# Moving the input normalisation of a gated recurrence from VectorE to ScalarE, with its statistics one step ahead

## What is computed

```python
h = layernorm(x) * (1 + ca) + sa
u = h @ W_in + b_in
gate_x, gate_a = sigmoid(u @ W_gx + b_gx), sigmoid(u @ W_ga + b_ga)
log_a = -8.0 * gate_a * softplus(a_param)
a, scale = exp(log_a), sqrt(1 - exp(2 * log_a))
# along the sequence: h_t = a_t * h_(t-1) + scale_t * gate_x_t * u_t
x = x + ga * (h @ W_out + b_out)
h = layernorm(x) * (1 + cb) + sb
x = x + gb * experts(h)
```

## Time and profile before

| | before |
|---|---|
| median of 3 runs | 1151.97 us (1151.54 to 1152.62) |
| the profiled execution, its own time | 1154.08 us |
| its span (first to last instruction) | 1152.3 us |
| PE busy | 1069.4 us, 93% |
| DVE / ACT / POOL busy | 746.0 / 759.1 / 430.4 us |
| mean granted TensorE clock | 0.962 |

### The profile page before, as it was taken

The page is one execution under the profiler, slowest core; times in us unless marked ns, Lnnn a source line. Parts: engine busy times, 40 slices in busy tenths (PEclk is TensorE's granted clock), DMA queues, the critical chain, the costliest instruction groups (busy, mean ns, idle before and its releaser), DMA issues.

```text
span 1152.3 us, 18801 instructions
## 1 busy us (share of the span) xinstructions
PE 1069.4 (93%) x6986; PEld 943.6 (82%) x6986; DVE 746.0 (65%) x1744; ACT 759.1 (66%) x1196; POOL 430.4 (37%) x387
## 2 busy tenths in 40 slices
PE   7899899999948999989999999999999999999993
PEld 6777777877736888879998899889998899888883
DVE  4779879989837888885535545354544554456565
ACT  4665647667427778877657776677667766776661
POOL 2121112112131445445445444445354444534532
PEclk8999989999867999999999999999999999999997
DMA  6035424121028445544434323433244332468971
GB/s 224 0 94 200 146 74 113 38 74 38 19 75 130 116 116 148 125 111 124 117 47 83 81 53 74 87 81 90 43 96 71 82 87 40 86 184 262 270 280 73
DMA packets 88442, 122.45 MB, mean 106 GB/s; under 512 B 17056, under 2 KB 74016, under 8 KB 87328
## 3 DMA queue, kind: packets, MB, share of 16 engines
q1 hardware_dynamic: 62960, 84.11, 23.2%
q0 software_dynamic: 24576, 36.37, 17.7%
q10 hardware_dynamic: 816, 0.79, 0.2%
HBM read 78.96 MB, written 42.27 MB: 105 GB/s over the span
## 4 chain that ended last, share of the span: by engine, by line
PE 59%; DVE 6%; ACT 2%; issue 2%; POOL 1%; DMA 0%; POOLq 0%; ACTq 0%; DVEq 0%
PE psum L1806 29%; PE psum L1831 26%; PE psum L1782 2%; DVE w_raw L1650 1%; DVE hidT L1696 1%; DVE scratch L1654 1%; PE psum L420 1%; DVE w L1644 1%; ACT rows_in L1587 1%; ACT hf L1610 1%; POOL out_x L1517 1%; DVE place L402 0%; ACT acc L1569 0%; DVE res_t L1654 0%; DMA out_x<-scratch 0%
## 5 line engine op out<-in xcount | busy, mean ns | idle before, releaser
L1806 PE MATMUL psum<-w,hidT 128*128 128x256 f32 x3072 | 375.1, 284 | 11.3 <-DVE hidT L1696 11.3
L1806 PEld LDWEIGHTS psum<-w,hidT 128*128 128x128 f32 x3072 | 367.3, 192 | 13.3 <-DVE hidT L1696 13.0
L1831 PE MATMUL psum<-xT,w 128*128 128x512 f32 x1536 | 372.2, 398 | 0.3 <-DVE xT L1683 0.3
L1696 DVE TENSOR_TENSOR hidT<-hf,hidT 128x512 fp32r<-128x512 f32 x256 | 175.4, 691 | 260.4 <-ACT hidT L1614 260.3
L1831 PEld LDWEIGHTS psum<-xT,w 128*128 128x128 f32 x1536 | 285.7, 190 | 59.7 <-DVE xT L1683 0.7
L1489 POOL DMA_INDIRECT ffn_rows<-rows_y,idx_cur x120 | 206.5, 1721 | 227.4 <-issue 167.8
L440 POOL DMA_INDIRECT rows_in<-x_rows,idx_cur x128 | 139.1, 1087 | 187.3 <-DVE idx_cur L413 152.7
L1558 ACT ACTIVATE rows_y<-psum,g_cur 128x256 f32<-128x256 f32 x128 | 53.8, 470 | 191.2 <-PE psum L1806 191.2
L1614 ACT ACTIVATE hidT<-hf 128x512 fp32r<-128x512 f32 x256 | 161.8, 632 | 8.1
L1610 ACT ACTIVATE hf<-psum 128x512 f32<-128x512 f32 x256 | 151.0, 590 | 22.1 <-PE psum L1831 13.1
L694 POOL TENSOR_SCALAR ve<-x 128x4 f32<-128x4 f32 x16 | 3.7, 229 | 221.3 <-DVE x L841 221.3
(11 more groups left out here) (205 smaller groups left out, 1238.9 us busy)
## 6 DMA issues: line engine op xcount, KB each, us to landing
w_raw<-in_L_ffn_w SPq DMA_DIRECT2D x30, 1024.0 KB, 6.0
x_rows<-x SPq DMA_DIRECT2D x16, 516.0 KB, 4.0
x_buf<-in_L_attn_x SPq DMA_DIRECT2D x16, 512.0 KB, 5.9
ffn_rows<-scratch SPq DMA_DIRECT2D x8, 1024.0 KB, 8.3
w_raw<-ffn_rows SPq DMA_DIRECT2D x16, 512.0 KB, 9.3
scratch<-x_rows SPq DMA_DIRECT2D x12, 512.0 KB, 7.1
out_x<-scratch SPq DMA_DIRECT2D x12, 512.0 KB, 4.2
rows_in<-x_rows,idx_cur POOLq DMA_INDIRECT x136, 2.9
```

The lines of the kernel that those rows point to most:

```text
L1696: dve.tensor_tensor(hidT[1][:, m, :], hf[m % HF][:], hidT[0][:, m, :].bitcast(F32), ALU.subtract).then_inc(f_hl, 1)
L1806: ins = pe.matmul(y_tile(u, t), hidT[qs][:, k, t * P:(t + 1) * P], w2_s[n % 2][qm][:, k, :], start=(x_ == 0), stop=(x_ == len(terms) - 1))
L1831: ins = pe.matmul(H_bank[m % 4], w1_s[n % 2][qs][:, k, m * P:(m + 1) * P], xT[qm][:, k, :], start=(x_ == 0), stop=(x_ == len(terms) - 1))
```

## The change

From group 5 on (`ON_DVE = 5`) the rows are normalised by ACT in place of DVE: four ACTIVATE Identity of 128x256 with scale rstd and bias -mean*rstd, after `keep_x1T` and before `gate_a` of the step whose group a it is. The statistics of such a group are taken one step earlier, in the same place of the DVE step; step 4 takes those of groups 4 and 5, step 15 none. POOL's `rstd1` moves with them and gets two more instructions, for the bias. SP loads group s+2 in step s, and there are six x buffers. The new tiles `nm1` are 16 bytes per partition each and the new x buffer 4096 bytes; they stand ahead of z1 and the buffers behind it. `roots_until` gives the semaphore count that belongs to the mixed number of instructions.

```diff
--- before.py
+++ after.py
@@ -455,7 +455,8 @@
             return recur.enter_context(nc.sbuf_tensor(name, shape, dt))
 
         LAST = NG + 3
-        XR = 5
+        XR = 6
+        ON_DVE = 5
 
 
         SETUP = KD * NMOD * D
@@ -506,6 +507,7 @@
         mv1 = [sbr(f"mv1_{n}", [P, TT, 2]) for n in range(2)]
         ve1 = sbr("ve1", [P, TT])
         rs1 = [sbr(f"rs1_{n}", [P, TT]) for n in range(2)]
+        nm1 = [sbr(f"nm1_{n}", [P, TT]) for n in range(2)]
         z1 = [sbr(f"z1_{n}", [P, TT, D]) for n in range(2)]
         sbr("apart_z", [P, 48])
         hT_z = [sbr(f"hT_z{q}", [P, KD, GT], F32R) for q in range(2)]
@@ -591,6 +593,10 @@
         r_sr = sem("scores_scaled")
         r_se = sem("scores_kept")
 
+        def roots_until(g):
+
+            return 2 * g + 2 * max(g - ON_DVE, 0)
+
         PAIR_AT, ROUNDS_IN = GB + 4, 4
         assert ROUNDS_IN * (NG - PAIR_AT) - BITS == 2
 
@@ -630,12 +636,13 @@
                 sp.dma_start(W_raw["out"][:], W_out.rearrange("(k p) n -> p k n", p=P)).then_inc(s_w["out"], 16)
                 sp.dma_start(bout_bc[:], b_out.rearrange("(o n) -> o n", o=1).to_broadcast([P, D])).then_inc(s_bo, 16)
                 load_mod("gb", 5, 1)
+                load_x(2)
 
                 acc_flat = [t.rearrange("(p r) d -> p (r d)", p=P) for t in acc_dram]
                 for s in range(1, LAST + 1):
                     _, _, _, d, _ = stages(s)
-                    if s + 1 < NG:
-                        load_x(s + 1)
+                    if s + 2 < NG:
+                        load_x(s + 2)
                     if s == 6:
                         sp.wait_ge(s_row, 2)
                         sp.wait_ge(s_mod, 3)
@@ -682,9 +689,17 @@
                     pool.wait_ge(r_mv1, g + 1)
                     if g >= 2:
                         pool.wait_ge(r_z1, g - 1)
+                    at = roots_until(g)
+                    if g >= ON_DVE:
+                        pool.wait_ge(r_rs1, at)
                     pool.tensor_scalar(ve1[:], mv1[g % 2][:, :, 1], EPS, None, ALU.add).then_inc(r_rs1, 1)
-                    pool.wait_ge(r_rs1, 2 * g + 1)
+                    pool.wait_ge(r_rs1, at + 1)
                     pool.tensor_tensor(rs1[g % 2][:], ve1[:], mhalf[:], ALU.pow).then_inc(r_rs1, 1)
+                    if g >= ON_DVE:
+                        pool.wait_ge(r_rs1, at + 2)
+                        pool.tensor_tensor(ve1[:], mv1[g % 2][:, :, 0], rs1[g % 2][:], ALU.mult).then_inc(r_rs1, 1)
+                        pool.wait_ge(r_rs1, at + 3)
+                        pool.tensor_scalar(nm1[g % 2][:], ve1[:], -1.0, None, ALU.mult).then_inc(r_rs1, 1)
 
                 def rstd2(g):
 
@@ -715,8 +730,10 @@
                         pool.memset(ones[:], 1.0).then_inc(q_con, 1)
                     if d is not None:
                         rstd2(d)
-                    if a is not None:
-                        rstd1(a)
+                    if s < ON_DVE:
+                        rstd1(s)
+                    if ON_DVE <= s + 1 < NG:
+                        rstd1(s + 1)
                     if s == NG + 2:
                         fetch(pool, 0)
                 fetch(pool, 1)
@@ -755,6 +772,16 @@
                     if g >= 1:
                         act.wait_ge(r_S, g)
                     act.activation(x1T[:], psX[:], ACT.Copy).then_inc(r_x1T, 1)
+
+                def norm1(g):
+
+                    act.wait_ge(r_rs1, roots_until(g + 1))
+                    act.wait_ge(r_z1, g)
+                    act.wait_ge(r_T1, g - 1)
+                    for t in range(TT):
+                        ins = act.activation(z1[g % 2][:, t, :], x_buf[g % XR][:, t, :], ACT.Identity, bias=nm1[g % 2][:, t:t + 1],
+                                             scale=rs1[g % 2][:, t:t + 1])
+                    ins.then_inc(r_z1, 1)
 
                 def gate_a(g):
 
@@ -802,7 +829,7 @@
                     act.activation(out[:], psO[:].rearrange("p h (q d) -> p (h q) d", d=D), ACT.Copy).then_inc(s_rk, 1)
 
                 for s in range(1, LAST + 1):
-                    _, c_, _, _, e_ = stages(s)
+                    a, c_, _, _, e_ = stages(s)
                     if c_ is not None:
                         hi_z(c_)
                     if s == 2:
@@ -811,6 +838,8 @@
                         keep_rows(2, gb_bc)
                     if e_ is not None:
                         keep_x1T(e_)
+                    if a is not None and a >= ON_DVE:
+                        norm1(a)
                     if c_ is not None:
                         gate_a(c_)
                         if s == PAIR_AT:
@@ -850,7 +879,7 @@
 
                 def norm1(g):
 
-                    dve.wait_ge(r_rs1, 2 * g + 2)
+                    dve.wait_ge(r_rs1, roots_until(g + 1))
                     if g >= 2:
                         dve.wait_ge(r_T1, g - 1)
                     for t in range(TT):
@@ -1083,8 +1112,10 @@
                     bits(n[1], n[2])
                     if s == NG:
                         chosen.ties()
-                    if a is not None:
-                        stats1(a)
+                    if s < ON_DVE:
+                        stats1(s)
+                    if ON_DVE <= s + 1 < NG:
+                        stats1(s + 1)
                     if s == 1:
                         dve.wait_ge(s_silu, 1)
                         dve.tensor_copy(spread[:], silu_c[:].unsqueeze(3).to_broadcast([P, KD, B, P])).then_inc(s_spr, 1)
@@ -1096,8 +1127,8 @@
                     bits(n[2], n[3])
                     if s == NG:
                         chosen.select()
-                    if a is not None and s > 2:
-                        norm1(a)
+                    if 2 < s < ON_DVE:
+                        norm1(s)
                     if s == 1:
                         score_weights()
                     if s == 2:
```

## The result

| | before | after |
|---|---|---|
| median | 1152.3 us (4 runs) | 1135.54 us (4 runs, 1131.69 to 1137.23) |
| ratio to before | | 0.985, 95% interval 0.9834 to 0.9867 |
| profiled execution, its span | 1154.08, 1152.3 us | 1134.41, 1132.6 us |
| mean granted clock | 0.962 | 0.968 |

Timed again beside other kernels, the same code gave 1136.22 us and a ratio of 0.9864 (0.9847 to 0.9881). So it is 1.4 to 1.5% faster, 16 to 17 us; the forecast was 15.1 us and 1136.9.

What follows compares the result with a forecast made beforehand. PE sets the pace except at step changes, where it waits for DVE's scores. 8.6 + 2.0 + 1.8 + 1.4 + 1.5 - 0.2 = 15.1 us off 1154.08 gives 1139.0, and 1136.9 as median; range 1133 to 1143.5.

Steps and rivals of the forecast that it cites:

- the term of steps 10 to 16: PE's waits for the scores at the starts of steps 10 to 16 vanish: 8.6 us gained.
- The overlap of 0.17 us: Where nothing holds PE, the transposes start 0.17 us before the listed end of the product; added to each vanished wait.
- Steps 5 and 7: Waits at the starts of steps 6 and 8 vanish, 2.0 and 1.4 us; no clock fall in step 7, 1.5 us.
- Step 6: At the start of step 7 PE's wait shrinks from 2.44 to about 0.8 us: 1.8 us gained.
- ScalarE at no cost: Four ACTIVATEs of 2.07 us fit ACT's gap ahead of `gate_a`, no table load: cost 0, seen only from 5 us.
- POOL, SP and placement at nothing: POOL's extra operations, SP's earlier loads and the moved buffers cost 0; 2% for placement kept as an end.
- Step 4: Takes the statistics of two groups on DVE, mostly within its waiting for POOL: -0.2 us.
- another time of the second block: Sign of being wrong: the second block, forecast to move as a whole, takes another time than before.
- Step 16 and the tail: The tail was to move as a whole with the second block: 0 in the sum.
- The rival of the clock: Step 8's clock falls shorter or not at all, 1134 us, or step 7 falls all the same, 1138.5; chance 0.15.
- DVE stays in the way: Rival: `gated_u` or `scale_w_out` delays DVE's chain at step changes; about 6 us less gain, 1143 us; chance 0.14.
- ACT's excess: Rival: the four ACTIVATEs outgrow ACT's gap, the first Tanh is late, PE follows; with 6 us, 1148; chance 0.04.

Runs made afterwards that it cites:

- Two passes: The changed kernel with the normalisation on ScalarE done twice, a semaphore between the passes: 1135.1 us, ratio 0.9846.
- three: The changed kernel with the normalisation on ScalarE done three times, with a semaphore between the passes: 1149.29 us, ratio 0.9971.
- the placement alone: The kernel before with six row buffers, the two unused bias tiles and loads two groups ahead, nothing else: 1150.68 us, ratio 0.9993.

## Why the prediction was right

- **What bounds, and the term of steps 10 to 16**: right, 8.64 us against 8.6 and a step of 16.31 us against 16.3. The overlap of 0.17 us read from one hand-over without a wait carried 1.2 us of it. It holds at the starts of all steps from 6 on but that of step 7.
- **Steps 5 and 7** (the waits at the starts of 6 and 8): 1.93 against 2.0, and 2.91 against 1.4 + 1.5. The clock didn't fall in step 7. Of the twelve profiled executions it fell there in the three that wait 2.36 to 2.44 us ahead of it and in none of the nine with 2.06 us or less. I had expected this from a single fall, and that it came true is in part luck: in other steps the length of the wait doesn't tell, as the last section shows.
- **Step 6**, 2.25 against 1.8, was mis-sized. I let DVE's clip follow PE by only 1.4 of 1.84 us, with the 0.62 us of waiting ahead of the clip as the cap. DVE does lag in this step: `gated_u` now starts 0.71 us after PE (104.92 less 104.21), where it started with it, since it waits 1.01 us for ACT's Sqrt. But the lag is taken out of those 0.62 us, and the clip comes nearly as long after the step's start as before (116.46 less 104.94 is 11.52 us, and 115.83 less 104.21 is 11.62). I counted the wait as a cap where it was the cushion. Of the 0.8 us of waiting that I had left at the start of step 7 some 0.3 remain.
- **ScalarE at no cost**: right, 2.07 us as in the earlier trace rows, no table load, and the room behind it is 2.93 us (forecast 3). Two passes are free, three are not.
- **POOL, SP and placement at nothing**: right. The six buffers and the loads alone give 0.9993, and POOL's busy time in the step rises from 3.35 to 3.79 us, with its result wanted a step later.
- **Step 4**, -0.2: step 4 takes 18.52 us for 18.32, as forecast. The other 1.0 us before step 5 was not in the sum. It stands ahead of step 4: 0.5 in the setup (the first x lands later: the first statistics start at 8.40 for 7.91), 0.3 in step 1, and the 0.2 in steps 2 and 3 that the buffers and loads alone show too. The second profile of the same kernel starts step 1 at 13.44, earlier than before, and step 1 takes 17.97 us there, 18.59 in the first and 18.31 before. So the 0.8 are a matter of the execution; what delays it in one and not in another stays open.
- **The experts' block**, 3.8 us, is no effect of the change that the profiles show: the second profile of the same kernel has 809.11 us. The prediction named another time of the second block as a sign that it is wrong. The sign came and says nothing, since identical code moves by more. Nine profiled executions of other kernels with the same experts' block give 805.7 to 810.1 us for it. The slow end and the fast end, measured from its first transposes (columns as in the earlier trace rows):

```profile
341.97:1152.30 810.33, 773.95 (x5383) 694.80 (x5383) 477.53 (x978) 564.05 (x938) 362.98 (x264) 0.97 0.47 112
```

```profile
337.71:1143.40 805.69, 768.26 (x5383) 690.28 (x5383) 477.02 (x978) 563.74 (x938) 366.30 (x264) 0.98 0.46 113
```

  The first is the kernel before, the second the one with three passes, which is slower as a whole. The instructions are the same in number, DVE's and ACT's busy times agree within 0.5 us, and PE's is 5.7 us longer at the lower clock (0.97 for 0.98). I read the difference as short stretches at 1.2 GHz, without having added them all up. Two of them in the kernel before, the clock is the third number from the right:

```profile
1044.00:1048.00 4.00, 4.00 (x23) 4.00 (x23) 3.93 (x7) 0.86 (x1) 0.00 (x0) 0.62 0.92 303
1072.00:1076.00 4.00, 4.00 (x21) 3.99 (x21) 3.54 (x4) 0.87 (x1) 0.00 (x0) 0.57 0.94 327
```

  and the changed kernel 16 us earlier, where the same work stands:

```profile
1028.00:1032.00 4.00, 4.00 (x35) 4.00 (x35) 3.90 (x8) 1.30 (x3) 0.00 (x0) 1.00 0.91 327
1056.00:1060.00 4.00, 4.00 (x38) 4.00 (x37) 1.83 (x3) 0.84 (x2) 0.62 (x1) 1.00 1.01 377
```

  Against the mean of all twelve profiled executions, 808.5, the one before was 1.8 us on the slow side and the one after 2.0 on the fast side. The scatter of whole executions goes with the clock too: beside the first experiments the kernel before was timed 19 times, from 1147.81 us with a mean granted clock of 0.968 to 1155.75 with 0.960.
- **Step 16 and the tail**, 1.2 us, were at 0 in the sum. The tail's projection waits 2.18 us for DVE in both profiles, and then runs three of its four groups slowly in the one and two in the other. The first group before (granted clock 0.50) and after (0.99):

```profile
312.44 1.91 PE L1242 MATMUL psum<-Wout,hs 128*128 128x256 f32 x4
```

```profile
297.59 1.03 PE L1273 MATMUL psum<-Wout,hs 128*128 128x256 f32 x4
```

  The length of this fall differs from profile to profile. But the stretch takes 54.9 to 55.1 us in the three kernels that don't take the statistics ahead and 53.6 to 53.9 in seven of the nine profiles that do (54.4 and 55.1 in the others). Whether that is chance or an effect of the change is not shown.

So the sum of 15.1 was right for what the change does, 15.9 between the starts of steps 5 and 16 less 0.2 in step 4, and the profile that it started from had a slow experts' block, which the step from 1154.08 to the median allowed for. That the median came out within 1.4 us of the forecast is in part luck: 1.0 us lost before step 4 and 1.2 won in the tail, neither of them in the sum, cancel. The medians differ by 16.8 and 16.6 us in the two timings, 1 us more than the steps give. The rival of the clock, to which I gave 0.15, is no other outcome but a scatter on top of every outcome: I had put it into the range through steps 7 and 8 alone, and taken the 1.1 us between three runs as a sign that it is small; the 19 timings spread over 7.9 us, and the experts' block, seven tenths of the time, moves by 4.6. The range held it by its other ends. Of the other rivals, "DVE stays in the way" had 0.14: it is what the statistics ahead without ScalarE do, and it doesn't happen with it. ACT's excess was tested up to its edge, and the placement alone.

## What to carry to other kernels

When an engine waits at a seam of a pipeline, read what stands behind the named instruction in program order, not what it computes: here PE waited for scores because a normalisation and its wait for POOL stood before them in DVE's list. Moving work to an engine with a gap was free in these runs up to the size of the gap, with its inputs ready when the gap begins; taking the inputs one step ahead was worth more than half of the gain by itself, and without it the move, to a later place, cost 1.5%. And before a gain of one percent is attributed, compare stretches of identical code in the two traces; what differs there is the scatter.

## What was not expected of the hardware

The fall of TensorE's clock doesn't follow from the length of the wait before it alone. After a wait of 0.98 us in step 8 the Wu product took 4.41 us in one kernel and 3.02 in another. After 2.66 or 2.7 us of waiting step 8 took 21.75, 21.56, 20.39 and 20.37 us. Step 3 of the changed kernel, with the same wait of 2.47 us for ACT each time, took 15.88 us in one profile and 17.58 in the second, where the clock fell; in the ten other kernels, with a wait of 2.47 us (2.62 in one), it took 15.8 to 16.0. The third group of four matmuls of the projection, from the first profile (granted clock 1.00) and from the second (0.50):

```profile
59.61 1.03 PE L1273 MATMUL psum<-Wout,hs 128*128 128x256 f32 x4
```

```profile
58.89 1.91 PE L1273 MATMUL psum<-Wout,hs 128*128 128x256 f32 x4
```

The Trainium skill says in "TensorE: Matmul & The Clock Gate", part 1, that the monitor's window runs freely and isn't reset at a kernel's start, so the number of slow matmuls depends on the phase. The traces agree in what they show, the same gaps, and falls that come, shorten or stay away; the phase itself stands in none of them. A fall cost 1.7 us in step 3, 1.3 in step 2 and 1.4 in step 8 behind the short wait. Behind the long wait of step 8 it is 1.7 to 3.1 us by estimate, against the 17.02 us without a fall and 1.7 of waiting more. The extremes of the experts' block are 4.6 us apart.
